# Products with stationary activations: down and output projections of a fused spiking-attention, FFN and attention block

## The chip, the cores and the metric

One core of one Trainium2 chip runs the kernel. The metric is the device time of the whole program in microseconds (us), the median of several runs; lower is better.

## The reference

The input x has 8 batches of 256 tokens of 128 features. Four blocks follow each other, each with a residual:

```
x = x + attn_a(layernorm(x))   # sigmoid projections, a matrix A from mean spike times, A @ V @ Wo + bo
x = x + ffn(layernorm(x))      # (silu(x wg) * (x wu)) wd, integer weights / 127
x = x + attn_b(layernorm(x))   # 16 heads of 64, causal softmax
x = x + ffn(layernorm(x))      # the same weights again
```

The two products that the change touches:

```
return jnp.einsum('bsh,dh->bsd', h, wd)            # ffn, h has 384 features: the down projection
out = jnp.einsum('bsha,had->bsd', z, Wo) + bo      # attn_b: the output projection
```

## The kernel before

All work is cut by batch b (0 to 7). Each batch goes through lnt and qkv, mean, vwo, aout (attn_a, letter A), lntF, gF0 to gF2, dnF, dbF (the first FFN, letter F), lntB, qk, v, scores, exp, transposes, sum, otA, otB, otr (attn_b, letter B; m = 8b + u counts the head pairs of all batches), and lntP, gP, dnP, dbP (the second FFN, letter P). Jobs of several batches are in flight together. Nothing schedules them at run time: `ORDER` is a table that lists, for each of TensorE, ScalarE, VectorE and GpSimd, every job in the order in which that engine runs it, and `BANKS` gives each job's PSUM bank. `full` waits until a job has filled its bank, `freed` until its reader has emptied it, `take` on TensorE until the bank's turn before is over. An engine that waits holds up everything behind it in its list. The SP queue loads x and stores each batch after dbP has been added (L392).

Much of the work on TensorE is done on values that are split in two fp32r parts, hi (rounded by ScalarE) and lo (the rest, by VectorE or GpSimd), for which a matmul is issued each time. `hot` jobs are four transposes of the identity with no result that is used.

Down projection (dnF, dnP; L463 to L471): the weight tile wd is stationary and 256 tokens of the hidden values stream past, hi and lo for each of the 3 chunks of features, six matmuls. Out come features on partitions and tokens on columns. ScalarE copies them to `dnt` (L690), and dbF or dbP (L486) turns them back by two transposes; VectorE then adds the result to x (L842). Two of the sixteen, F of batch 0 and P of batch 7 (`DIRECT`), take the hidden values as the stationary operand in plain fp32 (L480).

Output projection of batches 0 to 6: otA takes head pairs 0 to 3 and otB the pairs 4 to 7, three matmuls of 256 tokens for each pair:

```
nc.tensor.matmul(out[:, 0:N], wo_hi[:, u, :], z_hi, start=(u == 0), stop=False)
nc.tensor.matmul(out[:, 0:N], wo_lo[:, u, :], z_hi, start=False, stop=False)
last = nc.tensor.matmul(out[:, 0:N], wo_hi[:, u, :], z_lo, start=False, stop=(u == U - 1))
```

ScalarE copies the bank to `ot` (L700), otr transposes it twice (L534), VectorE adds it to x (L854). The last batch has its own product in plain fp32, tokens on partitions (pre0, pre1, out0, out1).

In the trace a plain fp32 product leaves two matmul records and two load records for each instruction, an fp32r product or a transpose one. Loads of the stationary operand are told as PEld.

## Time and profile before

| | |
|---|---|
| time, median of 3 runs | 320.98 us (320.28 to 321.02) |
| span of the profiled execution | 318.3 us |
| busy: TensorE, its loads | 307.6 us (97%), 268.4 us (84%) |
| busy: VectorE, ScalarE, GpSimd | 278.0 us (87%), 248.9 us (78%), 227.9 us (72%) |
| chain that ended last: TensorE, GpSimd, issue | 72%, 13%, 7% |

The profile shows one execution. Its own time is told as its span alone, from the first instruction to the last; the runs' median lies 2.7 us above it. A matmul's duration reaches from its start to the end of its last column, and the next one starts before that, so durations of TensorE don't add up; the distance from one start to the next does.

### The profile page before, as it was taken

To read this page: it belongs to the slowest core of one execution; us is meant where nothing else is said; L and a number is where in the kernel's file an instruction comes from. 1 tells how busy PE (TensorE), PEld (TensorE's weight loads), DVE (VectorE), ACT (ScalarE), POOL (GpSimd) and SP (SyncE) were. 2 spreads that over 40 slices of the span, in tenths; PEclk is the share of its full clock that TensorE was granted. 3 is DMA by queue.
4 is the path that set the end of the run, shared out by engine and by line. 5 is a ranking of instruction groups with operands and counts; after the bars stand their busy time and mean duration, and the time that the engine had idled before them with its cause. 6 is when DMAs were issued, how large, how long until landed. Compare 5 with 4: busy or idle time off the path is not lost.

```text
span 318.3 us, 10097 instructions
## 1 busy us (share of the span) xinstructions
PE 307.6 (97%) x3186; PEld 268.4 (84%) x3186; DVE 278.0 (87%) x1117; ACT 248.9 (78%) x848; POOL 227.9 (72%) x305
## 2 busy tenths in 40 slices
PE   6898999999999999999999999999999999999995
PEld 5687987988888898898888897888978998888884
DVE  4698999999899989997999989989998898998564
ACT  2665599899779798869889886998779788779832
POOL 4465786949978976977995489863977497646740
PEclk9999999999999999999999999999999999999999
DMA  7900000000000000000000000000000000000001
GB/s 201 316 7 0 3 0 4 2 3 1 2 2 2 2 2 4 0 3 3 18 2 3 3 16 3 2 18 3 2 1 4 19 0 21 2 2 4 2 0 49
DMA packets 6419, 5.83 MB, mean 18 GB/s; under 512 B 864, under 2 KB 5856, under 8 KB 6368
## 3 DMA queue, kind: packets, MB, share of 16 engines
q1 hardware_dynamic: 6080, 4.99, 5.2%
q8 instruction: 26, 0.43, 0.6%
q14 instruction: 25, 0.20, 0.2%
q10 hardware_dynamic: 288, 0.20, 0.2%
HBM read 4.15 MB, written 1.05 MB: 16 GB/s over the span
## 4 chain that ended last, share of the span: by engine, by line
PE 72%; POOL 13%; issue 7%; DVE 5%; DMA 1%; ACT 1%; POOLq 0%; DVEq 0%; ACTq 0%
PE bank L606 10%; PE bank L399 8%; PE bank L400 7%; PE bank L583 7%; PE bank L401 7%; PE bank L571 7%; POOL prob L1019 6%; PE bank L568 4%; PE bank L469 3%; PE bank L459 3%; PE bank L460 2%; PE bank L417 2%; PE bank L448 2%; PE bank L526 2%; PE bank L527 2%
## 5 line engine op out<-in xcount | busy, mean ns | idle before, releaser
L1019 POOL TENSOR_TENSOR prob<-prob,row_inv 128x256 f32<-128x256 f32 (+1 forms) x128 | 103.5, 838 | 33.9 <-DVE row_inv L921 33.8
L719 ACT ACTIVATE prob<-neg_s,neg_max 128x256 f32<-128x256 f32 x128 | 64.1, 501 | 0.0
L717 ACT ACTIVATE prob<-neg_s,neg_max 128x128 f32<-128x128 f32 x128 | 50.8, 397 | 13.8 <-DVE neg_max L897 13.2
L897 DVE CUSTOM_DVE_ANT_0 neg_s<-bank,mask 128x256 f32<-128x256 f32 x128 | 53.7, 420 | 0.0
L606 PE MATMUL bank<-early,v 128*64 128x256 f32 (+1 forms) x512 | 46.0, 330 | 0.1
L606 PEld LDWEIGHTS bank<-early,v 128*64 128x64 f32 x512 | 32.2, 137 | 13.1 <-issue 3.4
L931 DVE TENSOR_TENSOR qk<-bank,bqk 128x512 f32<-128x512 f32 x64 | 42.0, 681 | 0.9 <-PE bank L401 0.8
L571 PE MATMUL bank<-qk 64*128 64x256 f32 x256 | 38.6, 377 | 0.0
L895 DVE CUSTOM_DVE_ANT_0 neg_s<-bank,mask 128x128 f32<-128x128 f32 x128 | 36.4, 284 | 1.8 <-PE bank L571 1.7
L399 PE MATMUL bank<-rt_hi,wqkv_hi 128*128 128x256 f32 x128 | 37.2, 290 | 0.1
L400 PE MATMUL bank<-rt_hi,wqkv_lo 128*128 128x256 f32 x128 | 36.1, 282 | 0.0
L401 PE MATMUL bank<-rt_lo,wqkv_hi 128*128 128x256 f32 x128 | 36.1, 282 | 0.0
L906 DVE COPY early<-bank 128x384 f32<-128x384 f32 x64 | 32.9, 549 | 2.9 <-PE bank L583 2.8
L728 ACT ACTIVATE early<-bank 128x384 f32<-128x384 f32 x64 | 28.5, 488 | 7.6 <-PE bank L583 7.0
L583 PEld LDWEIGHTS bank<-ident,prob 64*128 64x128 f32 x768 | 27.7, 139 | 5.5 <-issue 2.2
L583 PE MATMUL bank<-ident,prob 64*128 64x64 f32 x768 | 30.9, 225 | 0.2 <-POOL prob L1019 0.2
L568 PE MATMUL bank<-qk 64*128 64x128 f32 x256 | 27.5, 291 | 0.2 <-issue 0.2
L568 PEld LDWEIGHTS bank<-qk 64*128 64x128 f32 x256 | 22.3, 187 | 4.5 <-issue 1.9
L399 PEld LDWEIGHTS bank<-rt_hi,wqkv_hi 128*128 128x128 f32 x128 | 24.3, 190 | 1.4 <-issue 0.5
L717 ACT ACTIVATION_READ_ACCUMULATOR prob<-neg_s,neg_max 128x1 f32 x128 | 24.8, 194 | 0.0
L400 PEld LDWEIGHTS bank<-rt_hi,wqkv_lo 128*128 128x128 f32 x128 | 24.3, 190 | 0.5
L719 ACT ACTIVATION_READ_ACCUMULATOR prob<-neg_s,neg_max 128x1 f32 x128 | 24.6, 192 | 0.0
(178 smaller groups left out, 887.2 us busy)
## 6 DMA issues: line engine op xcount, KB each, us to landing
early<-wqkv_in SPq DMA_DIRECT2D x3, 512.0 KB, 6.9
x<-x_in SPq DMA_DIRECT2D x8, 128.0 KB, 5.7
out<-x SPq DMA_DIRECT2D x8, 128.0 KB, 1.8
wo<-wo_in SPq DMA_DIRECT2D x1, 512.0 KB, 7.0
wa<-wa_in ACTq DMA_DIRECT2D x1, 192.0 KB, 3.1
first<-wg_in SPq DMA_DIRECT2D x1, 192.0 KB, 3.1
first<-wu_in SPq DMA_DIRECT2D x1, 192.0 KB, 3.1
first<-wd_in SPq DMA_DIRECT2D x1, 192.0 KB, 4.8
```

The costliest lines, as they stand in the source:

```text
L399: nc.tensor.matmul(out, w_hi_ap, r_hi_ap, start=True, stop=False)
L400: nc.tensor.matmul(out, w_lo_ap, r_hi_ap, start=False, stop=False)
L401: return nc.tensor.matmul(out, w_hi_ap, r_lo_ap, start=False, stop=True)
L568: nc.tensor.matmul(home(f"s{e}", m)[0][:, 0:P], qk[half, r, 0, 0:P], qk[half, r, 1, 0:P], start=True, stop=True)
L571: nc.tensor.matmul(S[:, P:SC], qk[half, r, 0, P:N], qk[half, r, 1, :], start=True, stop=True).then_inc(done, 1)
L583: last = nc.tensor.transpose(out[:, at:at + A], prob[half, m % PROB_BUFS, e, j * P:(j + 1) * P], ident[half, half])
L606: last = nc.tensor.matmul(out[half, t + k * P:t + N], v[:, b % 2, k, h * A:(h + 1) * A], transposed(i)[:, e, cols], start=(k == 0), stop=( ...
L717: nc.scalar.activation(prob[:, r, e, 0:P], neg_s[:, m % SCORE_BUFS, e, 0:P], ACT.Exp, bias=neg_max[:, q, 2 * e:2 * e + 1], scale=-1.0, acc ...
L719: nc.scalar.activation(prob[:, r, e, P:SC], neg_s[:, m % SCORE_BUFS, e, P:SC], ACT.Exp, bias=neg_max[:, q, 2 * e + 1:2 * e + 2], scale=-1. ...
L897: nc.vector.tensor_tensor_reduce(out=neg_s[:, m % SCORE_BUFS, e, P:SC], in0=S[:, P:SC], in1=mask[:], scale=-SCORE_SCALE, scalar=3e38, op0= ...
L931: nc.vector.tensor_tensor(qk[:, m % QK_BUFS, :, :], W[:].rearrange("p (w s) -> p w s", s=N), bqk[:, u, :].unsqueeze(2).to_broadcast([P, 2, ...
L1019: nc.gpsimd.tensor_tensor(pr, pr, inv, ALU.mult).then_inc(p_norm, 1)
```

## The change

The jobs dnF, dnP and otr are gone, with the copies of ScalarE and the tiles `dnt` and `ot`. dbF and dbP now wait for the split hidden values and compute the down projection themselves: for each half of the tokens and each chunk, the hi and the lo hidden tile is stationary (128 x 128) and wd streams with its 128 columns. otA and otB do the same with z_hi, z_lo as stationary tiles and wo_hi, wo_lo streaming. The results stand with tokens on partitions, and VectorE adds them to x from the bank. The hidden buffers are free for the next batch once db is done. All of ORDER and BANKS is new.

The end of TensorE's list, before, from the down projection of batch 6 of P (hid_hi_P) on:

```order
L469 MATMUL bank<-hid_hi_P,wd 128x256 x3
L469 MATMUL bank<-hid_lo_P,wd 128x256 x3
L486 MATMUL bank<-ident,dnt_P 128x128 x2
L499 MATMUL bank<-ident 128x128 x2
L500 MATMUL bank<-ident 128x128
L501 MATMUL bank<-ident 128x128
L486 MATMUL bank<-ident,dnt_P 128x128 x2
L480 MATMUL bank<-wd,hid_F 128x128 x6
```

The same place now:

```order
L487 MATMUL bank<-ident 128x128 x2
L488 MATMUL bank<-ident 128x128
L489 MATMUL bank<-ident 128x128
L473 MATMUL bank<-wd,hid_hi_P 128x128
L473 MATMUL bank<-wd,hid_lo_P 128x128
...
L464 MATMUL bank<-wd,hid_F 128x128 x6
```

The six wide matmuls and the transposes became twelve matmuls of 128 columns (the pair of L473 rows comes six times), and the projection of batch 5 left this place: it now stands between lntP.7 and gP0.7:

```order
L411 MATMUL bank<-ident,xn_F 128x128 x2
L473 MATMUL bank<-wd,hid_hi_P 128x128
L473 MATMUL bank<-wd,hid_lo_P 128x128
...
L453 MATMUL bank<-xt_hi_F,wg 128x256
```

GpSimd's list, before, around the split of the output weights (wo_lo), just ahead of the first output projection:

```order
L1003 TENSOR_TENSOR hid_lo_F<-hid_F,hid_hi_F 128x256
L1007 TENSOR_TENSOR wo_lo<-wo,wo_hi 128x1024
L991 TENSOR_SCALAR sv<-t_qkv 128x256
L986 TENSOR_TENSOR x<-x,bo_all 128x256
L1003 TENSOR_TENSOR hid_lo_F<-hid_F,hid_hi_F 128x256 x2
```

Now the split stands near the start of the kernel:

```order
L941 TENSOR_SCALAR xn_A<-x,mv_eps,rstd_A 128x128 x2
L978 TENSOR_TENSOR wo_lo<-wo,wo_hi 128x1024
L962 TENSOR_SCALAR sv<-t_qkv 128x256
L983 TENSOR_SCALAR stdp<-less 128x512
L967 TENSOR_TENSOR wqkv_lo<-early,wqkv_hi 128x512
L962 TENSOR_SCALAR sv<-t_qkv 128x256
```

It moved from after ten normalisations to before the first, and the splits of the query, key and value weights (wqkv_lo) now queue behind it.

```diff
@@ -49,148 +49,143 @@
 ORDER = {
     "PE": """
...
-        v3.0 scores.3 scores.4 scores.5 mean.2 v2.0 qk.6 dnF.1 qk.7 v0.0 dbF.1 transposes.0 transposes.1 transposes.2
...
 BANKS = {
-    "lntA": "43744110",
...
+    "lntA": "32277257",
...
-    "dnF": "06070106",
...
-    "ot": "5264737",
-    "otr": "3116311",
...
-    "dnP": "4514010",
...
+    "ot": "3362374",
...
@@ -281,7 +276,7 @@
         sv, tq, tk, vwo = sb("sv", [P, 2, N]), sb("tq", [P, 2, N]), sb("tk", [P, 2, T]), sb("vwo", [P, 2, T, D])
         dist, less = (sb(n, [P, T, N]) for n in ("dist", "less"))
         stdp, xb = sb("stdp", [P, 2, T, N]), sb("xb", [P, 2, T, D])
-        gate_t, hid, dnt = ({k: sb(f"{n}_{k}", [P, w, N]) for k in "FP"} for n, w in (("gate_t", FC), ("hid", FC), ("dnt", 1)))
+        gate_t, hid = ({k: sb(f"{n}_{k}", [P, FC, N]) for k in "FP"} for n in ("gate_t", "hid"))
         hid_hi, hid_lo = ({k: sb(f"{n}_{k}", [P, FC, N], F32R) for k in "FP"} for n in ("hid_hi", "hid_lo"))
         qk = sb("qk", [P, QK_BUFS, 2, N])
         v = sb("v", [P, 2, T, H * A])
@@ -291,7 +286,6 @@
         prob_t = early[:].rearrange("p (m e s) -> p m e s", m=PT_BUFS, e=2)
         zt_hi, zt_lo = sb("zt_hi", [P, Z_SLOTS, N], F32R), sb("zt_lo", [P, Z_SLOTS, N], F32R)
         wo_hi, wo_lo = sb("wo_hi", [P, U, D], F32R), sb("wo_lo", [P, U, D], F32R)
-        ot = sb("ot", [P, N])
         zt_last = first[:, 0:U * N].rearrange("p (u s) -> p u s", s=N)
 
         bank = [ctx.enter_context(nc.psum_tensor(f"bank{i}", [P, 512], F32)) for i in range(8)]
@@ -459,16 +453,6 @@
                         nc.tensor.matmul(out[:, cols], w[:, cs], xt_hi[buffers(k, b)][:, 0, :], start=True, stop=False)
                         last = nc.tensor.matmul(out[:, cols], w[:, cs], xt_lo[buffers(k, b)][:, 0, :], start=False, stop=True)
                     last.then_inc(done, 1)
-                elif job in ("dnF", "dnP"):
-                    k = job[2]
-                    for c in range(FC):
-                        pe.wait_ge(hl_s[k][c], turn_of(k, b))
-                    take(job, b)
-                    for half in (hid_hi, hid_lo):
-                        for c in range(FC):
-                            last = nc.tensor.matmul(out[:, 0:N], wd[:, c, :], half[k][:, c, :], start=(half is hid_hi and c == 0),
-                                                    stop=(half is hid_lo and c == FC - 1))
-                    last.then_inc(done, 1)
                 elif job in ("dbF", "dbP"):
                     k = job[2]
                     if (k, b) in DIRECT:
@@ -480,10 +464,14 @@
                                 last = nc.tensor.matmul(out[:, j * D:(j + 1) * D], hid[buffers(k, b)][:, c, j * P:(j + 1) * P], wd[:, c, :].bitcast(F32),
                                                         start=(c == 0), stop=(c == FC - 1))
                     else:
-                        freed(pe, f"dn{k}", b)
+                        for c in range(FC):
+                            pe.wait_ge(hl_s[k][c], turn_of(k, b))
                         take(job, b)
                         for j in range(T):
-                            last = nc.tensor.transpose(out[:, j * D:(j + 1) * D], dnt[k][:, 0, j * P:(j + 1) * P], ident[:])
+                            for c in range(FC):
+                                for half in (hid_hi, hid_lo):
+                                    last = nc.tensor.matmul(out[:, j * D:(j + 1) * D], half[k][:, c, j * P:(j + 1) * P], wd[:, c, :],
+                                                            start=(c == 0 and half is hid_hi), stop=(c == FC - 1 and half is hid_lo))
                     last.then_inc(done, 1)
                 elif job == "bo":
                     pe.wait_ge(bv_s, 1)
@@ -522,17 +510,13 @@
                     else:
                         freed(pe, "sum", U * b + U - 1)
                     for u in range(0 if first else U // 2, U // 2 if first else U):
-                        z_hi, z_lo = zt_hi[:, slot(b, u), :], zt_lo[:, slot(b, u), :]
-                        nc.tensor.matmul(out[:, 0:N], wo_hi[:, u, :], z_hi, start=(u == 0), stop=False)
-                        nc.tensor.matmul(out[:, 0:N], wo_lo[:, u, :], z_hi, start=False, stop=False)
-                        last = nc.tensor.matmul(out[:, 0:N], wo_hi[:, u, :], z_lo, start=False, stop=(u == U - 1))
+                        for j in range(T):
+                            z_hi, z_lo = (z[:, slot(b, u), j * P:(j + 1) * P] for z in (zt_hi, zt_lo))
+                            o = out[:, j * D:(j + 1) * D]
+                            nc.tensor.matmul(o, z_hi, wo_hi[:, u, :], start=(u == 0 and j == 0), stop=False, skip_group_check=True)
+                            nc.tensor.matmul(o, z_hi, wo_lo[:, u, :], start=False, stop=False, skip_group_check=True)
+                            last = nc.tensor.matmul(o, z_lo, wo_hi[:, u, :], start=False, stop=(u == U - 1), skip_group_check=True)
                     last.then_inc(ota_s if first else done, 1)
-                elif job == "otr":
-                    freed(pe, "ot", b)
-                    take(job, b)
-                    for j in range(T):
-                        last = nc.tensor.transpose(out[:, j * D:(j + 1) * D], ot[:, j * P:(j + 1) * P], ident[:])
-                    last.then_inc(done, 1)
                 elif job[0] == "v":
                     g, j = divmod(int(job[1]), T)
                     freed(pe, "lntB", b)
@@ -679,25 +663,12 @@
                     k, c = job[2], int(job[3])
                     freed(act, f"g{k}{c}", b)
                     if turn_of(k, b) > 1:
-                        full(act, f"dn{k}", b - 1)
+                        full(act, f"db{k}", b - 1)
                     nc.scalar.activation(hid_hi[k][:, c, :], hid[k][:, c, :], ACT.Copy).then_inc(hh_s[k][c], 1)
-                elif job in ("dnF", "dnP"):
-                    k = job[2]
-                    src, _, free = home(job, b)
-                    full(act, job, b)
-                    if turn_of(k, b) > 1:
-                        full(act, f"db{k}", b - 1)
-                    nc.scalar.activation(dnt[k][:, 0, :], src[:, 0:N], ACT.Copy).then_inc(free, 1)
 
                 elif job == "oh":
                     act.wait_ge(ld_b, 64)
                     nc.scalar.activation(wo_hi[:], wo[:], ACT.Copy).then_inc(woh_s, 1)
-                elif job == "ot":
-                    src, _, free = home(job, b)
-                    full(act, job, b)
-                    if b:
-                        full(act, "otr", b - 1)
-                    nc.scalar.activation(ot[:], src[:, 0:N], ACT.Copy).then_inc(free, 1)
                 elif job == "dist":
                     act.wait_ge(mean_s, b + 1)
                     if b:
@@ -772,7 +743,7 @@
                     if k == "A":
                         dve.wait_ge(ld_x[b], 16)
                     elif k == "P" and b < B - 1:
-                        freed(dve, "otr", b)
+                        freed(dve, "ot", b)
                     elif k == "P":
                         freed(dve, "out0", b)
                         freed(dve, "out1", b)
@@ -847,7 +818,7 @@
                     full(dve, job, b)
                     dve.wait_ge(xbo_s, b + 1)
                     nc.vector.tensor_tensor(x[:, j, :], src[:, 0:D], x[:, j, :], ALU.add).then_inc(free, 1)
-                elif job == "otr":
+                elif job == "ot":
                     src, _, free = home(job, b)
                     full(dve, job, b)
                     dve.wait_ge(xbo_s, b + 1)
@@ -999,7 +970,7 @@
                     k, c = job[2], int(job[3])
                     pool.wait_ge(hh_s[k][c], turn_of(k, b))
                     if turn_of(k, b) > 1:
-                        full(pool, f"dn{k}", b - 1)
+                        full(pool, f"db{k}", b - 1)
                     nc.gpsimd.tensor_tensor(hid_lo[k][:, c, :], hid[k][:, c, :], hid_hi[k][:, c, :].bitcast(F32), ALU.subtract).then_inc(hl_s[k][c], 1)
 
                 elif job == "ol":
```

## Rows read from the trace of the kernel before

**Rows 1.** the page of the profile: span, busy time of each engine, clock, the chain by engine

```profile
span 318.3 us, 10097 instructions
...
PE 307.6 (97%) x3186; PEld 268.4 (84%) x3186; DVE 278.0 (87%) x1117; ACT 248.9 (78%) x848; POOL 227.9 (72%) x305
...
PEclk9999999999999999999999999999999999999999
...
PE 72%; POOL 13%; issue 7%; DVE 5%; DMA 1%; ACT 1%; POOLq 0%; DVEq 0%; ACTq 0%
```

**Rows 2.** groups of instructions by form, TensorE: line, operation, tiles, count, busy us, mean ns

```profile
L526 PE MATMUL bank<-zt_hi,wo_hi 128*128 128x256 f32 x56 | 16.1, 288 | 0.3 <-POOL wo_lo L1007 0.3
...
L469 PE MATMUL bank<-hid_hi_F,wd 128*128 128x256 f32 x21 | 3.9, 296 | 0.0
...
L534 PE MATMUL bank<-ident,ot 128*128 128x128 f32 x14 | 2.8, 284 | 0.0
```

**Rows 3.** timeline of TensorE, sixth output projection: start us, us, engine, line, form

```profile
252.13 0.28 PE L526 MATMUL bank<-zt_hi,wo_hi 128*128 128x256 f32 x1
...
254.88 0.28 PE L528 MATMUL bank<-zt_lo,wo_hi 128*128 128x256 f32 x1
```

**Rows 4.** timeline of TensorE, a down projection of the second FFN near the end

```profile
306.25 0.52 PE L469 MATMUL bank<-hid_hi_P,wd 128*128 128x256 f32 x3
...
306.60 0.52 PE L469 MATMUL bank<-hid_lo_P,wd 128*128 128x256 f32 x3
...
306.96 0.28 PE L459 MATMUL bank<-xt_hi_P,wg 128*128 128x256 f32 x1
```

**Rows 5.** timeline of TensorE, transposes of the identity near the end

```profile
308.63 0.38 PE L499 MATMUL bank<-ident 128*128 128x128 f32 x2
...
308.85 0.27 PE L500 MATMUL bank<-ident 128*128 128x128 f32 x1
```

**Rows 6.** timeline around a mean's product: TensorE's matmuls, then its weight loads

```profile
44.15 0.50 PE L432 MATMUL bank<-mean_w,t_qkv 128*128 128x1 f32 x4
...
44.51 0.49 PE L399 MATMUL bank<-wqkv_hi,rt_hi 128*128 128x512 f32 x1
...
44.84 0.40 PE L400 MATMUL bank<-wqkv_hi,rt_lo 128*128 128x512 f32 x1
...
45.07 0.40 PE L401 MATMUL bank<-wqkv_lo,rt_hi 128*128 128x512 f32 x1
...
44.48 0.19 PEld L399 LDWEIGHTS bank<-wqkv_hi,rt_hi 128*128 128x128 f32 x1
...
44.60 0.19 PEld L400 LDWEIGHTS bank<-wqkv_hi,rt_lo 128*128 128x128 f32 x1
```

**Rows 7.** timeline, the direct down projection at the end, weight loads

```profile
313.95 1.41 PEld L480 LDWEIGHTS bank<-wd,hid_F 128*128 128x128 f32 x12
```

**Rows 8.** groups of instructions by form, ScalarE: count, busy us, mean ns

```profile
L690 ACT ACTIVATE dnt_F<-bank 128x256 f32<-128x256 f32 x7 | 2.7, 382 | 1.4 <-PE bank L469 1.4
...
L700 ACT ACTIVATE ot<-bank 128x256 f32<-128x256 f32 x7 | 2.7, 382 | 1.5 <-PE bank L528 1.5
```

**Rows 9.** the chain that ended last: start us, us, what

```profile
74.47 2.38 POOL wo_lo L1007
...
311.96 0.94 PE bank L469 x6
...
313.75 0.41 PE bank L486 x2
...
314.16 1.41 PE bank L480 x12
```

**Rows 10.** timeline of the probabilities' loads, a weight split of GpSimd, TensorE's fifth query/key product

```profile
296.65 1.81 PEld L583 LDWEIGHTS bank<-ident,prob 64*128 64x128 f32 x48 [0.17 <-issue]
...
21.68 1.29 POOL L996 TENSOR_TENSOR wqkv_lo<-early,wqkv_hi 128x512 fp32r<-128x512 f32 x1
...
37.69 0.28 PE L399 MATMUL bank<-rt_hi,wqkv_hi 128*128 128x256 f32 x1
```

More of the change, by code:

```diff
@@ L81 @@
[L81 to L82 removed]
+        hot.0 hot.1 hot.2 hot.3 hot.4 hot.5 hot.6 hot.7 hot.8 lntA.0 qkv1.0 qkv0.0 qkv2.0 mean.0 hot.9 hot.10 hot.11 hot.12
+        lntA.1 vwo.0 aout.0 hot.13 hot.14 qkv1.1 qkv0.1 qkv2.1 lntF.0 mean.1 gF0.0 gF2.0 gF1.0 bo.0 lntA.2 dbF.0 qkv2.2 qkv1.2
+        vwo.1 vwo.2 aout.1 lntB.0 qkv0.2 qk.0 qk.1 qk.2 scores.0 scores.1 scores.2 lntF.1 qk.3 qk.4 gF0.1 gF1.1 gF2.1 v1.0 qk.5
@@ new lines @@
+        v0.0 scores.3 scores.4 scores.5 transposes.0 mean.2 qk.6 qk.7 dbF.1 v3.0 transposes.1 lntA.3 transposes.2 sum.1
+        transposes.3 scores.6 scores.7 v2.0 aout.2 lntB.1 sum.3 qkv1.3 qk.8 qk.9 qk.10 v3.1 qk.11 v0.1 transposes.4 transposes.5
+        transposes.6 transposes.7 scores.8 scores.9 scores.10 qkv0.3 qk.12 qkv2.3 qk.13 lntF.2 sum.5 scores.11 gF2.2 v1.1 gF1.2
+        sum.7 scores.12 scores.13 qk.14 mean.3 gF0.2 otA.0 otB.0 qk.15 vwo.3 transposes.8 transposes.9 dbF.2 v2.1 transposes.10
@@ new lines @@
+        scores.14 scores.15 transposes.11 sum.9 sum.11 lntA.4 lntB.2 aout.3 transposes.12 v2.2 qk.16 qk.17 qk.18 v0.2
+        transposes.13 scores.16 scores.17 sum.13 lntP.0 lntF.3 qk.19 v1.2 gP2.0 v3.2 gF1.3 transposes.14 transposes.15 scores.18
+        scores.19 qkv2.4 gF2.3 gF0.3 qkv1.4 sum.15 qk.20 qk.21 qkv0.4 qk.22 transposes.16 transposes.17 scores.20 scores.21
+        scores.22 dbF.3 gP1.0 gP0.0 otA.1 lntA.5 transposes.18 transposes.19 mean.4 otB.1 qk.23 lntB.3 sum.17 qk.24 vwo.4 qk.25
@@ new lines @@
+        transposes.20 transposes.21 scores.23 scores.24 scores.25 sum.19 sum.21 lntP.1 qk.26 qk.27 aout.4 v0.3 gP2.1 v1.3 dbP.0
+        qkv2.5 gP1.1 transposes.22 transposes.23 scores.26 transposes.24 scores.27 qk.28 qk.29 lntF.4 v2.3 qkv0.5 qk.30 qk.31
+        gF1.4 qkv1.5 gP0.1 scores.28 transposes.25 mean.5 gF2.4 gF0.4 otA.2 vwo.5 scores.29 sum.23 sum.25 scores.30 lntA.6 dbF.4
+        otB.2 qkv2.6 aout.5 transposes.26 transposes.27 scores.31 dbP.1 v3.3 lntB.4 sum.27 v2.4 qk.32 qk.33 transposes.28
@@ new lines @@
+        v1.5 gF2.6 qk.43 gF0.6 gP0.3 transposes.38 transposes.39 dbP.2 gF1.6 sum.37 sum.39 transposes.40 transposes.41 scores.42
+        scores.43 gP1.3 qkv1.7 qk.44 qk.45 dbF.6 qk.46 mean.7 scores.44 scores.45 gP2.3 qk.47 otA.4 otB.4 v3.5 vwo.7 lntB.6
+        scores.46 transposes.42 transposes.43 sum.41 transposes.44 scores.47 transposes.45 sum.43 aout.7 qk.48 qk.49 v1.6 lntP.4
+        scores.48 scores.49 qk.50 gP2.4 v2.6 qk.51 gP0.4 lntF.7 dbP.3 sum.45 transposes.46 transposes.47 scores.50 scores.51
```

232 lines of the change are left out of this document (106 added, 126 removed).

## The prediction

> **What bounds the kernel now.** I read the page's busy shares and chain first [rows 1]. TensorE is busy 97% of a span of 318.3 us, at the full granted clock all the way; VectorE follows at 87%, ScalarE at 78%, GpSimd at 72%. The busy share of TensorE overstates it, since the matmuls' durations overlap, but the chain that ended last says the same: 72% of it is TensorE's work, 13% GpSimd's, 7% "issue", and ScalarE's share is 1%. So a change is priced first by what it does to TensorE's stream.
>
> A duration in the groups [rows 2] is no price: a matmul of 256 columns is listed at 288 ns, but starts follow each other much more closely. The price is the distance from one start to the next (pitch). In one output projection 24 matmuls run unbroken, the first at 252.13, the last at 254.88: 2.75 us over 23 steps, **0.120 us** each [rows 3]. In one down projection six of them take from 306.25 to the next job's start at 306.96: **0.118 us** each [rows 4]. Transposes of 128 columns (here of the identity, the same form) come every **0.110 us**: two from 308.63 to 308.85 [rows 5].
>
> **The change, part by part.** Both products are turned round: the activations are the stationary operand, so the tokens come out on partitions and nothing is transposed back. The activation tile that is loaded has 128 tokens where 256 streamed, so each matmul of 256 columns becomes two of 128: 24 become 48 in each of seven output projections, 6 become 12 in each of fourteen down projections (batches 1 to 7 of F, 0 to 6 of P; the two direct ones stay). Two transposes for each of the 21 go. In all 504 matmuls of 128 columns stand where there were 168 + 84 of 256 columns and 42 transposes [rows 2].
>
> What one of the new ones costs is the question of this case, because no reduced-precision (fp32r) matmul here streams fewer than 256 columns. Nearest rows, from both sides:
> - Streaming alone. The 512-column matmuls of the value projection have a pitch of 0.23 us (44.84 to 45.07) [rows 6], against 0.120 at 256 columns. The straight line through both gives 0.120 - 0.5 x 0.11 = 0.063 us at 128 columns. That is the lower end.
> - Loading alone. Four matmuls of the mean stream **one** column each and still need 0.36 us from 44.15 to 44.51, 0.09 us each, where streaming would need next to nothing; and the two fp32r loads behind them start at 44.48 and 44.60, 0.12 apart [rows 6]. The direct down projection, 128 columns in full fp32, runs its twelve loads in 1.41 us, of which the last one's own duration is 0.19: (1.41 - 0.19)/11 = 0.111 us [rows 7].
> - The upper end of the same mechanism is today's 0.120 us: a narrower stream can't be slower than a wider one of its kind.
>
> So a new 128x128 load every matmul sets the pitch, and halving the columns buys nothing. I take **0.112 us** (that of the direct projection, the nearest in shape, rounded up) and keep 0.120 as the high end.
>
> Output projection: 48 x 0.112 = 5.38 us; before 24 x 0.120 + 2 x 0.110 = 3.10. Plus 2.28, seven times: **+15.9 us**. Down projection: 12 x 0.112 = 1.34; before 6 x 0.118 + 2 x 0.110 = 0.93. Plus 0.41, fourteen times: **+5.8 us**. Together +21.7. At 0.120 it is 2.66 x 7 + 0.51 x 14 = +25.8.
>
> The Trainium skill, "TensorE: Matmul & The Clock Gate", section "Back-to-back issue gap", gives a sustained spacing of about 81 ns for pairs of load and matmul at 128 columns. By it the 504 would take 40.8 us, and TensorE's work would grow by 6.1 us instead of 21.7. The loads here come no closer than 0.11 us [rows 6, 7], so the trace speaks for the dearer figure.
>
> ScalarE loses 21 evacuations of 382 ns [rows 8], 8.0 us of its 248.9. It holds 1% of the chain, so this is worth nothing by itself. The cover is TensorE's queue, and TensorE gets longer. VectorE still adds each result to x from a bank (the same 21 instructions), now released by the projection itself. The chain of a projection gets shorter by an evacuation and two transposes; in the middle of the kernel the engine runs another job meanwhile, so this hop was hidden. 21 turns of banks fewer are needed, which can only ease the waits for a bank. The SP queue's stores wait on the same job as before.
>
> At the end it isn't hidden. From 311.96 the chain holds six matmuls (0.94), two transposes, and an evacuation with its hops up to 313.75, two more transposes (0.41), then the direct projection at 314.16: 2.20 us [rows 9]. Now twelve matmuls stand there: 1.34 + about 0.2 of start, 1.6 us; the twelve of the batch before moved ahead of the last gate products, where TensorE turned idle matmuls over while it waited for a split. **-0.5 us**.
>
> The orders: GpSimd's split of the output weights (wo_lo) was on the chain at 74.47 for 2.38 us just ahead of the first projection [rows 9]; it moves into the first 25 us. There a copy of sv, a step of stdp and two weight splits queue behind it; the first of these splits ran at 21.68, and TensorE first reads it at 37.69 [rows 10], so 2.4 us more are covered (without that cover they would be paid in full). That is worth 0 to 2.4; I take **-1.0**, because other work of GpSimd takes its place on the chain. All other moves are small and of both signs, I give them 0 with 2 us on either side.
>
> **How much of +21.7 reaches the end.** If TensorE were the whole chain, all of it. It is 72% [rows 1]; the other 28% are waits on normalisation, splits and issue, and part of them is covered once TensorE runs later than the others. With the chain's share as the lower rate, 15.6; with all of it, 21.7. The inserted blocks themselves are unbroken TensorE work on the chain [rows 3, 9], so I take it nearer to the full rate, 20.3. Sum: 20.3 - 0.5 - 1.0 = **+18.8 us**. On the profiled span that is 318.3 + 18.8 = 337.1; the runs' median of 320.98 lies 2.7 above the span, and the difference carries over: **339.8 us**.
>
> **Rivals.**
> 1. *Half-width reduced matmuls run as plain fp32.* Every 128-column product in this trace is plain fp32 and leaves two matmul records for each instruction (12 in the chain's last row for the direct projection's six [rows 9]), 0.224 us for the pair. Should the single pass hold only for wide tiles, 504 x 0.224 = 112.9 us against 34.7 before: +78.2, with the credits of 1.5 some 398 us. For it: no narrow fp32r matmul exists here to say otherwise. Against it: records are split by type, and both widths that are shown take one. Chance 0.10.
> 2. *The loads hide, and streaming decides* (the other side). Place: every load of the 504. Price: at the 0.063 us of the straight line 31.8 us against 34.7, -2.9; with -0.5 and -1.0 it comes to 316.6 us. It decides from a pitch of 34.7/504 = 0.069 us down. For it: the 48 loads of the probabilities' transposes, on half the rows each, come every 0.04 us [rows 10], and two matmuls in each three of the output projection hold the same stationary tile. Against it: the one-column rows, and the tail's identity transposes, which repeat the same tile and still come at 0.110 [rows 5]. Chance 0.07. The skill's formula in that same section, columns over 2.4 GHz plus 2.5 ns, would make it 56 ns and 28.2 us, so faster still by 3.6 us; the one-column rows, at a multiple of it, do not agree.
> 3. *Only the repeated tile is kept.* A third of the 336 output matmuls (112) would skip the load: 112 x (0.112 - 0.063) = -5.5 us, 334.3 us. Inside the range, by part of the main case.
> 4. *The waits swallow it.* TensorE grows but VectorE and GpSimd were due anyway: two thirds of 21.7 vanish in today's waits, 7.2 - 1.5 = +5.7, 326.7 us. For it: VectorE's 87%. Against it: the chain is at VectorE in only 5% [rows 1]. Chance 0.07.
>
> **Numbers.** Load-bound, as worked out (rival 3 within it): 0.76, between 329 (pitch 0.112, chain's rate 15.6, the moves at their best, the repeated tile kept: 15.6 - 5.5 x 0.72 - 0.5 - 2.4 - about 1 = +8) and 347 (25.8 in full, no credit). To hold 8 in 10 the range reaches down to rival 4's 326. About 0.3% is what a measurement of this kernel can tell from no change, that is 320.0 to 321.9. Faster: rival 2, 0.07. Within: edges of rivals 2 and 4, 0.03. Slower: the rest, 0.90.
>
> **What the profile after would show.** 504 matmuls of 128x128 at the two projections, each with its own load; a pitch of 0.11 to 0.12 in an unbroken block (5.4 us for 48, where 2.9 stood); no matmul or activation on the lines that are gone; TensorE's share of the chain up by some points; ScalarE's busy time near 241 us; wo_lo off the chain. A pitch at or under 0.07, or two records for each instruction, proves the step wrong, and then rival 2 or 1 holds. A pitch of 0.112 with a span under 327 would leave the step of the rate at fault.

## The result, and the profile after

The changed kernel takes **343.65 us** (median of 4 runs, 343.19 to 344.35) beside 321.0 for the kernel before on the same chip: a ratio of 1.0714, 95% interval 1.0702 to 1.0727. It is slower by 22.7 us; 339.8 was forecast, with a range of 326 to 347.

The page of the changed kernel, where [rows 1] stood before:

```profile
span 341.4 us, 10455 instructions
...
PE 328.3 (96%) x3396; PEld 288.6 (85%) x3396; DVE 278.4 (82%) x1117; ACT 245.8 (72%) x827; POOL 227.7 (67%) x305
...
PE 89%; POOL 5%; issue 2%; DVE 2%; ACT 1%; POOLq 0%; DVEq 0%; ACTq 0%
```

TensorE was 72% of the chain that ended last and is 89% now. The span grew by 23.1 us, TensorE's busy time by 20.7; the other engines do what they did (ScalarE 3.1 us less) and are idle for longer. TensorE's clock is granted in full all the way (1.00).

The groups by form, matmuls and then weight loads (these answer to [rows 2]):

```profile
L517 PE MATMUL bank<-wo_lo,zt_hi 128*128 128x128 f32 x112 | 30.8, 275 | 0.0
...
L473 PE MATMUL bank<-wd,hid_hi_P 128*128 128x128 f32 x42 | 9.8, 276 | 0.5 <-POOL hid_lo_P L974 0.5
```

```profile
L517 PEld LDWEIGHTS bank<-wo_lo,zt_hi 128*128 128x128 f32 x112 | 21.5, 192 | 0.0
```

Three such groups of 112 and four of 42 make the 504. One record stands for each instruction, so these products run as a single pass and not as plain fp32. L517 follows L516 with the same stationary tile z_hi and still has its own 112 loads.

The timeline of TensorE through the first output projection gives the price (before: [rows 3]); 48 matmuls, the last one followed by a query/key product:

```profile
78.92 0.22 PE L516 MATMUL bank<-wo_hi,zt_hi 128*128 128x128 f32 x1
78.98 0.28 PE L517 MATMUL bank<-wo_lo,zt_hi 128*128 128x128 f32 x1
79.09 0.27 PE L518 MATMUL bank<-wo_hi,zt_lo 128*128 128x128 f32 x1
79.20 0.28 PE L516 MATMUL bank<-wo_hi,zt_hi 128*128 128x128 f32 x1
...
84.12 0.28 PE L518 MATMUL bank<-wo_hi,zt_lo 128*128 128x128 f32 x1
84.23 0.33 PE L393 MATMUL bank<-rt_hi,wqkv_hi 128*128 128x256 f32 x1
```

From 78.92 to 84.23 are 5.31 us for 48: a pitch (the distance from one start to the next) of **0.111 us**, though each duration is listed as 275 ns. A down projection near the end runs from 330.92 to 332.29, 1.37 us for twelve. Per projection that is 5.31 - 3.10 = 2.21 us more, seven times 15.5; and 1.37 - 0.93 = 0.44 us more, fourteen times 6.2. Together 21.7, the sum that the prediction had for TensorE. It is scaled up from one block of each kind; a count of all blocks, further down, comes to 20.6.

The waits of the other engines, by what they wait for:

```profile
POOL prob L990 <- DVE row_inv L892: 48.3, 29, 5.6
ACT early L699 <- PE bank L567: 18.9, 20, 2.7
...
DVE x L825 <- PE bank L518: 11.6, 7, 3.3
```

GpSimd's first wait was 33.8 us before and ScalarE's wait for the transposes 7.0; VectorE now waits up to 3.3 us for an output projection. These three engines stand idle for longer in all, and 89% of the chain is TensorE's.

Where the time is added shows in four marks, read off the timelines in us: the start of TensorE's first scores, of its first output projection, of its last sum product, and from that to the end.

| kernel | first scores | first output projection | last sum | tail |
|---|---|---|---|---|
| before | 33.84 | 76.89 | 301.21 | 17.06 |
| changed | 34.76 | 78.92 | 323.61 | 17.78 |

The tail is what is left behind the start of the last sum product. Up to the first scores 0.9 us are added, from there to the first output projection 1.1, from there to the last sum product 20.4, in the tail 0.7.

### The profile page after: what moved, and what is told of

Read it like the earlier page. It is cut to its first block, busy times and chain, and to the rows that moved or that the text cites. A ratio compares the mean times of both kernels' runs of the same rounds, so it can differ in the third digit from the quotient of the medians.

```text
span 341.4 us, 10455 instructions
## 1 busy us (share of the span) xinstructions
PE 328.3 (96%) x3396; PEld 288.6 (85%) x3396; DVE 278.4 (82%) x1117; ACT 245.8 (72%) x827; POOL 227.7 (67%) x305
## 4 chain that ended last, share of the span: by engine, by line
PE 89%; POOL 5%; issue 2%; DVE 2%; ACT 1%; POOLq 0%; DVEq 0%; ACTq 0%
PE bank L590 13%; PE bank L393 8%; PE bank L567 8%; PE bank L555 8%; PE bank L394 7%; PE bank L395 7%; PE bank L473 6%; PE bank L552 5%; PE bank L518 4%; PE bank L517 4%; PE bank L516 4%; PE bank L453 3%; PE bank L454 3%; PE bank L411 2%; PE bank L442 2%
## 5 line engine op out<-in xcount | busy, mean ns | idle before, releaser
L590 PE MATMUL bank<-early,v 128*64 128x256 f32 (+1 forms) x512 | 46.7, 330 | 0.1
L902 DVE TENSOR_TENSOR qk<-bank,bqk 128x512 f32<-128x512 f32 x64 | 42.8, 685 | 4.3 <-PE bank L395 3.7
L699 ACT ACTIVATE early<-bank 128x384 f32<-128x384 f32 x64 | 29.2, 488 | 19.4 <-PE bank L567 18.9
L393 PE MATMUL bank<-rt_hi,wqkv_hi 128*128 128x256 f32 x128 | 37.9, 296 | 0.6 <-DVE rt_lo L839 0.6
L877 DVE COPY early<-bank 128x384 f32<-128x384 f32 x64 | 33.6, 551 | 5.2 <-PE bank L567 4.6
L567 PE MATMUL bank<-ident,prob 64*128 64x64 f32 x768 | 32.1, 226 | 0.0
L518 PE MATMUL bank<-wo_hi,zt_lo 128*128 128x128 f32 x112 | 30.8, 275 | 0.0
L517 PE MATMUL bank<-wo_lo,zt_hi 128*128 128x128 f32 x112 | 30.8, 275 | 0.0
L516 PE MATMUL bank<-wo_hi,zt_hi 128*128 128x128 f32 x112 | 30.5, 272 | 0.0
L552 PEld LDWEIGHTS bank<-qk 64*128 64x128 f32 x256 | 21.7, 187 | 4.8 <-issue 3.1
```

What stands on the lines that cost most here:

```text
L393: nc.tensor.matmul(out, w_hi_ap, r_hi_ap, start=True, stop=False)
L517: nc.tensor.matmul(o, z_hi, wo_lo[:, u, :], start=False, stop=False, skip_group_check=True)
L552: nc.tensor.matmul(home(f"s{e}", m)[0][:, 0:P], qk[half, r, 0, 0:P], qk[half, r, 1, 0:P], start=True, stop=True)
L567: last = nc.tensor.transpose(out[:, at:at + A], prob[half, m % PROB_BUFS, e, j * P:(j + 1) * P], ident[half, half])
L590: last = nc.tensor.matmul(out[half, t + k * P:t + N], v[:, b % 2, k, h * A:(h + 1) * A], transposed(i)[:, e, cols], start=(k == 0), stop=( ...
```

## The experiments

Each is given as its edit, what was expected, what was measured, and what follows. Times are medians; ratios are to the kernel before on the same chip, with their 95% interval.

### Is it the load? Smaller loads against narrower streams

Two edits of the changed kernel leave its 504 matmuls and all orders alone. One halves what is loaded (64 tokens, A = 64), the other halves what streams.

```diff
-   matmul(out[:, j * D:(j + 1) * D], half[k][:, c, j * P:(j + 1) * P], wd[:, c, :], ...)
+   matmul(out[0:A, j * D:(j + 1) * D], half[k][:, c, j * P:j * P + A], wd[:, c, :], ...)   # e4, z_hi and z_lo alike
+   matmul(out[:, j * D:j * D + D // 2], half[k][:, c, j * P:(j + 1) * P], wd[:, c, 0:D // 2], ...)   # e5, wo_hi and wo_lo alike
```

**Half the load (e4).**

> The changed kernel with 64 instead of 128 tokens in each stationary tile of the 504, streaming 128 columns as changed; it leaves out the other 64 tokens of each tile. Load theory: the load halves, the pitch falls from 0.112 to the streaming value of about 0.063 us: -24.7 us on TensorE, 319 to 325 us, and the pitch in a block is 0.06 to 0.07. Rival, a fixed cost for each matmul (issue) of 0.112 whatever it loads: 343 to 344 us and an unchanged pitch.

Measured 319.06 us (318.88 to 319.17), ratio 0.9958 [0.9943, 0.9972]: 24.6 us less than the changed kernel. The timeline of the same place:

```profile
79.20 0.22 PE L516 MATMUL bank<-wo_hi,zt_hi 128*64 128x128 f32 x1
79.26 0.23 PE L517 MATMUL bank<-wo_lo,zt_hi 128*64 128x128 f32 x1
79.32 0.22 PE L518 MATMUL bank<-wo_hi,zt_lo 128*64 128x128 f32 x1
```

With the same count and the same 128 columns the pitch fell from 0.111 to 0.06 us, and the time stands at the low edge of what was expected if the load decides. 504 x 0.051 = 25.7 us of TensorE, and 24.6 of it came off the time. Whether the smaller load or the 128 columns set the 0.06 can't be told: the straight line for the stream alone lies at nearly the same place.

**Half the stream (e5).**

> The changed kernel streaming only 64 of the 128 weight columns in each of the 504 matmuls, with the full 128x128 tile loaded each time; it leaves out half of the features of both products. Load theory: nothing changes, 343.0 to 344.3 us, pitch 0.11. Rival, the stream still decides some of the pitch (half of 504 x 0.056): 14 us less, 329 us; it decides at once between load and stream, as e4 did between load and issue.

Measured 362.92 us, and from 355.67 to 367.35 over the runs at a mean granted clock of 0.93 to 0.96; the ratio for the two runs at 0.95 and 0.96 is 1.1153 [1.1113, 1.1193]. The expectation was missed by far, but not by its mechanism. The timeline of the first block, and three stretches around it (length, each engine's busy time, then the granted clock before the DMA share):

```profile
79.40 0.28 PE L517 MATMUL bank<-wo_lo,zt_hi 128*128 128x64 f32 x1
79.51 0.28 PE L518 MATMUL bank<-wo_hi,zt_lo 128*128 128x64 f32 x1
...
81.52 0.28 PE L518 MATMUL bank<-wo_hi,zt_lo 128*128 128x64 f32 x1
...
81.97 0.40 PE L518 MATMUL bank<-wo_hi,zt_lo 128*128 128x64 f32 x1
82.19 0.40 PE L516 MATMUL bank<-wo_hi,zt_hi 128*128 128x64 f32 x1
```

```profile
79.30:81.70 2.40, 2.40 (x25) 2.40 (x23) 2.33 (x9) 2.21 (x7) 2.31 (x4) 1.00 0.00 0
81.70:98.80 17.10, 17.10 (x109) 15.54 (x108) 6.62 (x24) 6.12 (x22) 7.87 (x12) 0.50 0.00 1
98.80:110.00 11.20, 11.20 (x126) 9.20 (x124) 9.83 (x44) 7.98 (x26) 7.84 (x11) 1.00 0.01 1
```

Up to 81.5 us, at the full 2.4 GHz, the pitch is 0.11 us (79.40 to 81.52 in 19 steps, 0.112): half the columns bought nothing. Then, inside the block, the clock is granted at its half level (1.2 GHz), the pitch doubles to 0.21, and it stays so for 17.1 us. This happens seven times in the run. An estimate of what the clock took: time at half rate is half lost, so a run loses (1 - mean granted clock) x span, and without it the four spans come to 339.7 to 340.1 us, close to the changed kernel's 341.4. So the pair of runs says: **the load of a 128x128 stationary tile sets the pitch; neither the stream nor the issuing of an instruction does.** The clock is taken up again below.

### Is it the count, or the new orders?

**Cut in two (e2).** The kernel before with its own orders, banks and orientation; only each matmul of 256 columns at the two products is cut into two of 128.

```diff
-   matmul(out[:, 0:N], wo_hi[:, u, :], z_hi, ...)
+   for j in range(T):
+       matmul(out[:, j * P:(j + 1) * P], wo_hi[:, u, :], z_hi[:, j * P:(j + 1) * P], ...)   # and so the others
```

> The kernel before, orders, banks, copies and transposes untouched; each wide matmul of both products is cut in two of 128 streamed columns (weights stationary as before, loaded twice). Pitch theory: 504 x 0.112 = 56.4 us for 168 x 0.120 + 84 x 0.118 = 30.1 us, +26.3 us on TensorE, at nine tenths to the full rate: 345 to 347 us. Rival, that the orders carry the loss: well under 335 us. Streaming as the limit: 504 x 0.063 = 31.8, so 323 us.

Measured 345.26 us (345.12 to 345.36), ratio 1.0775 [1.0757, 1.0793]: +24.9. As expected: with nothing moved and nothing turned round, cutting alone costs more than the whole change does. The new orders are not the main cause.

**Half of the new matmuls (e3), and half of those of the down projections (e6).** The changed kernel with `for j in range(1)` in place of `range(T)`: in both products, and in the down projections alone.

> The changed kernel with the second half of the tokens left out of both products (252 of the 504 new matmuls), all other jobs, orders and banks as changed. It leaves out half of the down and output projections' results. Pitch theory: -28.2 us on TensorE, so 343.7 falls by 20 to 28, to 316 to 324 us (TensorE then has 6.5 us less to do than before, and other engines can bind). Rival, that orders or banks carry the loss: above 332 us.

> The changed kernel with the second half of the tokens left out of the fourteen down projections alone (84 of 168 matmuls). Pitch theory, at the rate of 0.96 that e3 showed for all 252: 84 x 0.112 x 0.96 = -9.0 us, 334.6 us (+-1). Rival: down projections stand where TensorE waits anyway, so much of it vanishes: above 338 us.

Measured 316.62 us (315.98 to 317.12), ratio 0.9881 [0.9863, 0.9899], and 334.1 us (333.88 to 334.5), ratio 1.0433 [1.042, 1.0447]. The first takes away 27.0 us for 252 x 0.112 = 28.2 of TensorE's work, 0.96 of it; the second 9.5 for 84 x 0.112 = 9.4, all of it. Both are inside what was expected. In e3's profiled run the clock stood at half from 306.3 to 309.7 us, and its tail is 17.78 us where e6's is 16.64, so 0.96 is rather too low. So nearly every microsecond that these blocks take arrives at the end.

**The output projection alone (e1).** The kernel before, with only otA and otB turned round as in the change (its bank row for ot new, ot's places on VectorE and the halves' places on TensorE moved by a few jobs); the down projections stay wide.

```diff
-    "ot": "5264737",
+    "ot": "1124337",
```

> The kernel before with the output projection alone turned round (48 matmuls of 128 columns for 24 of 256, otr and its copy gone); the down projections as before; before's orders with only the ot jobs' banks and places shifted so that the banks come free. Theory of TensorE's pitch: +2.28 us seven times, +15.9 us, nearly all of it at the end: 335 to 338 us. Rival, that the new orders and banks carry the loss: these are nearly the old ones here, so under 330 us.

Measured 340.26 us (339.89 to 340.46), ratio 1.0618 [1.0603, 1.0634]: +19.9, where its term is 15.5 to 15.9: above the range that was expected, by some 2 us, and 4 above the term. Its marks up to the first output projection (33.80, 76.86) and its tail (17.05) are those of the kernel before, so all of it arises in the middle. There TensorE's listed idle time rises from 0.5 to 2.1 us; where the rest of the 4 us arises was not located.

**The same, with half its matmuls (e11).**

```diff
-                        for j in range(T):
+                        for j in range(1):
```

> The kernel e1_out_only (output projection alone turned round, the orders of before with its new places and banks) with the second half of the tokens left out of the seven output projections, so half of their matmuls (168) are gone; rows 128 to 255 of each batch get wrong sums. TensorE then does 24 x 0.112 = 2.69 us per projection where before did 3.10, 2.9 us less in seven. Theory A, the 4 us that e1_out_only cost beyond its term are a fixed price of the places and banks that were patched for it: 340.3 less 0.95 to 1.0 of 18.8, so 321.4 to 322.5 us. Theory B, they arise only with the long blocks themselves (each holds up work on other engines that comes back late): with short blocks they vanish, 317.9 to 319.0 us, below before.

Measured 326.26 us (324.75 to 329.28), ratio 1.0176 [1.014, 1.0212]; the runs at full clock took 324.75 and 324.88. Theory B is refuted: with blocks shorter than those of the kernel before, this version is still slower than it. That speaks for the places and banks patched for e1. But A's fixed price of 4 us isn't shown either: its range was missed upward by more than 2 us, since taking matmuls away gave back 15.5 of 18.8 at full clock and no more, so that the price here would be nearer 7. What e1 costs beyond its term stays open in part. The down projections alone, on the orders of before, were not tried.

### The tail

The forecast had -0.5 us for the end on top of what the two down projections there add (0.8), so +0.3; it is +0.7. The changed kernel's timeline there, TensorE, ScalarE and GpSimd, with the idle time ahead in brackets:

```profile
330.71 0.44 PE L411 MATMUL bank<-ident,xn_F 128*128 128x128 f32 x2 [1.01 <-DVE xn_F L767]
...
332.55 0.73 ACT L667 ACTIVATE hid_hi_P<-hid_P 128x256 fp32r<-128x256 f32 x2 [0.98 <-PE bank L473]
...
333.40 2.11 POOL L974 TENSOR_TENSOR hid_lo_P<-hid_P,hid_hi_P 128x256 fp32r<-128x256 f32 x3 [3.39 <-ACT hid_hi_P L667]
...
335.77 0.30 PE L473 MATMUL bank<-wd,hid_hi_P 128*128 128x128 f32 x1 [0.52 <-POOL hid_lo_P L974]
```

There is one set of hidden tiles for P. Before, they were free once dnP of batch 5 had run, ahead of batch 6's gates. Now dbP of batch 5 reads them itself, at 330.92 to 332.29, and ScalarE's rounding for batch 6 waits for it (0.98 us), GpSimd's split waits for the rounding (3.39), and TensorE, which turns idle transposes over meanwhile, still waits 0.52.

**Batch 5's projection earlier (e7).**

```diff
-  gP1.6 hot.15 gP0.6 gP2.6 lntP.7 dbP.5 gP0.7
+  gP1.6 dbP.5 hot.15 gP0.6 gP2.6 lntP.7 gP0.7
```

> The changed kernel with the down projection of P batch 5 moved on TensorE from behind lntP.7 to behind gP1.6. Theory: batch 6's rounding (hid_hi_P) now waits until that projection has read the buffers, and through GpSimd's splits the last two projections start late; moved, dbP.6 starts about 1.2 us and dbP.7 about 1.0 us earlier: 342.4 to 342.9 us. Rival, the tail is bound by the last batch's own chain (xn, gates): 343.5 or above.

Measured 345.04 us (343.93 to 345.8), ratio 1.0771 [1.0752, 1.0789]; tail 18.10 against 17.78. The theory is a miss: the edit made it worse, and the time lies in the rival's range. Of the 0.7 us that the profiled span grew, 0.4 were there at the first output projection (79.34 against 78.92), far ahead of the edit: the clock stood at half for 3.4 us near the start (see the last section). The tail's share is 0.3, and TensorE's timeline shows why it got no shorter.

```profile
333.51 0.39 PE L453 MATMUL bank<-xt_hi_F,wg 128*128 128x256 f32 x1 [1.86 <-DVE xt_lo_F L839]
...
336.51 0.30 PE L473 MATMUL bank<-wd,hid_hi_P 128*128 128x128 f32 x1
```

Dropped ahead of the gates of batch 6, dbP of batch 5 pushes them back, and with them the work of ScalarE and VectorE that stands ahead of batch 7's normalised input (xt_lo). TensorE now waits 1.86 us for it at 333.51; in the changed kernel it was ready at 332.02, and its gates started at 332.29, right behind dbP of batch 5. The wait on the split is gone, but dbP of batch 6 starts 0.7 us later than it did. So most of that block of 1.3 us had filled a wait in its old place, and the edit took it out of there.

**The other way out (e9): batch 6 direct in the kernel before.** Down projection of P batch 6 in plain fp32 from the unsplit hidden values, as batch 7's; its rounding, split, copy and transposes back go, and it moves ahead of dbP of batch 5.

```diff
-DIRECT = {("F", 0), ("P", B - 1)}
+DIRECT = {("F", 0), ("P", B - 2), ("P", B - 1)}
-  gP0.7 gP1.7 gP2.7 dnP.6 dbP.5 hot.18 dbP.6 dbP.7
+  gP0.7 gP1.7 gP2.7 dbP.6 dbP.5 hot.18 dbP.7
```

> The kernel before with the down projection of P batch 6 made direct (plain fp32, hidden values stationary, no rounding, split, copy or transposes; six matmuls between the last gate products and the end). Theory: near the end the chain goes through GpSimd's splits of batch 6 (308.45 to 311.96) and a copy and two transposes; without them the last projection starts 0.5 to 0.9 us earlier: ratio 0.997 to 0.9985. Rival: the last batch's gates set the end, ratio 1.000.

Measured 320.09 us (319.75 to 320.51, 11 runs) beside 320.61 (21 runs), ratio 0.999 [0.9981, 0.9999]: hardly to be told from no change, and a little less than expected. Its chain ends so:

```profile
311.62 1.34 PE bank L480 x12
312.96 0.22 PE bank L486 x2
...
313.84 1.59 PE bank L480 x12
```

The chain no longer passes through a split or an evacuation behind the last gates. What lies between the two direct projections is TensorE's own queue: the two transposes back of batch 5 (L486) and the idle ones. Note the 1.34 us: six plain fp32 instructions, with twelve loads, take TensorE as long as the changed kernel's twelve matmuls on split values, without the split.

### The split of the output weights

The prediction moved wo_lo off the chain and credited 1.0 us. The chain of the changed kernel, in the head:

```profile
22.10 1.58 POOL xn_A L941 x2
23.69 2.34 POOL wo_lo L978
...
26.93 0.62 POOL stdp L983
27.55 1.24 POOL wqkv_lo L967
```

It is on the chain still. Behind it wait sv, stdp and the weight splits on GpSimd, and from there the chain goes on through the normalisations to TensorE at 37.06. Two runs put it elsewhere.

**Back to its old place (e8).**

```diff
-  lnsF.0 lnsA.2 ol.0 sv.1 ... norm.9 hlF2.2 xb.4
+  lnsF.0 lnsA.2 sv.1 ... norm.9 hlF2.2 ol.0 xb.4
```

> The changed kernel with GpSimd's split of the output weights moved back to where the kernel before has it (behind norm.9). Theory A: in the changed kernel it lies on the chain at 23.7 us for 2.3 us and delays the first heads by some 0.9 us; back in its place it costs the middle instead, where TensorE has more to do than before and hides it: 342.5 to 343.2 us. Theory B, that the move was worth the 1.0 us that the prediction gave it: 344.2 to 345 us.

Measured 351.79 us (350.68 to 355.15), ratio 1.1012 [1.0971, 1.1053]. Both theories missed, by some 7 us or more. TensorE's timeline, then stretches as above:

```profile
81.59 0.33 PE L506 MATMUL bank<-wo_hi,zt_hi 128*128 128x128 f32 x1 [2.12 <-POOL wo_lo L968]
...
83.43 0.28 PE L507 MATMUL bank<-wo_lo,zt_hi 128*128 128x128 f32 x1
...
83.66 0.41 PE L506 MATMUL bank<-wo_hi,zt_hi 128*128 128x128 f32 x1
83.88 0.41 PE L507 MATMUL bank<-wo_lo,zt_hi 128*128 128x128 f32 x1
```

```profile
80.00:83.60 3.60, 2.01 (x18) 2.01 (x19) 2.23 (x6) 3.45 (x11) 3.51 (x5) 1.00 0.00 0
83.60:93.90 10.30, 10.30 (x66) 9.96 (x65) 2.21 (x4) 0.70 (x3) 3.38 (x5) 0.50 0.01 2
93.90:110.00 16.10, 16.10 (x179) 13.31 (x179) 14.27 (x67) 12.16 (x41) 13.43 (x18) 1.00 0.01 2
```

TensorE stands still for 2.12 us, then runs a block of 128x128 loads with 128 columns each; after 2.0 us of it the clock is granted at half, and 10.3 us pass at half rate, the block's pairs at a pitch of 0.21. The same block without the wait ahead of it kept the full clock in the changed kernel. The wait costs 2 us, and half of the 10.3 us, 5, is the clock's. The marks agree: of the 7.5 us that the profiled span grew, 0.3 lie ahead of the first scores (35.10), 2.3 between them and the first output projection (81.59), and 4.8 between that and the last sum (331.12).

**Into an idle stretch (e12).**

```diff
-  lnsF.0 lnsA.2 ol.0 sv.1 ... norm.7 lnsF.2 norm.8
+  lnsF.0 lnsA.2 sv.1 ... norm.7 lnsF.2 ol.0 norm.8
```

> The changed kernel with GpSimd's split of the output weights moved out of the head into the stretch from 66.4 to 72.0 us in which GpSimd waits 5.60 us for a reciprocal (behind lnsF.2). Theory A, the split delays the head by 0.9 us and nothing waits for it here: 342.5 to 343.2 us, the milestone of the first scores back at 33.9 and no wait on wo_lo at the first output projection, so no fall of the clock there, other than in e8_wo_lo_back. Theory B, without the split in the head TensorE's clock falls to half near 22 us as in e8_wo_lo_back, which eats the gain: 343.3 to 344.5 us.

Measured 343.38 us (342.69 to 343.45), ratio 1.071 [1.0695, 1.0724], which can't be told from the changed kernel's 1.0714. The first scores start at 34.20, 0.56 earlier, and the first output projection at 78.43, 0.49 earlier, with no wait; GpSimd's timeline shows the split inside the old idle stretch, which was 5.60 us long:

```profile
65.85 2.39 POOL L978 TENSOR_TENSOR wo_lo<-wo,wo_hi 128x1024 fp32r<-128x1024 f32 x1
71.49 1.61 POOL L990 TENSOR_TENSOR prob<-prob,row_inv 128x256 f32<-128x256 f32 x2 [3.25 <-DVE row_inv L892]
```

Of the 0.9 us of the head a little more than half comes back. The median lies where B put it and not where A did, but B's mechanism is not there: the clock is 0.999 in the profiled run and 1.000 in the four others. A was right in kind and too large: the span is 0.5 us shorter than the changed kernel's, and the medians, 0.3 apart, can't tell it. Beside e8 the run shows that taking the split out of the head was not what cost 8 us there: the loss came with the wait for it and the fall of the clock behind that wait.

### A version that beats both (e10)

e9, and the same move of wo_lo into the kernel before, where GpSimd waits 4.07 us behind lnsF of batch 2:

```diff
-  norm.7 lnsF.2 norm.8 lnsA.4 norm.9
+  norm.7 lnsF.2 ol.0 norm.8 lnsA.4 norm.9
```

> As e9, and GpSimd's split of the output weights moved from behind norm.9 to behind lnsF.2, into 4.07 us in which GpSimd sat idle. Theory: the 2.38 us that it held on the chain at 74.47 go, and other work takes part of it: 0.5 to 2.4 us less than e9, ratio 0.990 to 0.997. Rival: the work behind it takes its place on the chain, no difference from e9.

Measured **319.72 us** (319.31 to 319.83, 11 runs) beside 320.61, ratio 0.9972 [0.9963, 0.9981]: faster than both kernels, by 0.9 us than the one before. It is 0.37 us below e9, where 0.5 to 2.4 was expected, so a little short of the range. The first output projection starts at 76.44, before it was 76.89; but from there to the last sum product it takes 224.7 us where the kernel before took 224.3, and what is left of the profiled gain is e9's shorter tail (16.71 against 17.06). The page's chain:

```profile
PE 91%; DVE 4%; issue 1%; DMA 1%; POOL 1%; ACT 1%; POOLq 0%; DVEq 0%
```

GpSimd's 13% of the chain [rows 1] are down to 1%, and the time fell by 0.3%: nearly all of GpSimd's share had lain beside TensorE's own work, which now stands on the chain instead.

## Why the prediction was right, point by point

**What bounds the kernel.** Right: TensorE's stream. e3 and e6 took away matmuls and got 0.96 to 1.0 of them back.

**The price of a new matmul, 0.112 us.** Right: 0.111 in the block, and e4 against e5 shows the reason given to be the true one. The nearest row had been the direct projection, 0.111 [rows 7]. All 21 projections of the changed kernel, each counted from its first matmul to the next job's, take 56.3 us, where 504 x 0.112 are 56.4.

**Output and down projections, +15.9 and +5.8.** From one block of each kind the measured growth is 15.5 and 6.2, and that sum agrees with the 21.7. Counted in the same way over all blocks of both traces, the output projections go from 20.7 to 37.4 us and the down projections from 10.6 to 18.9, and 4.4 us of transposes are gone: **+20.6**, and TensorE's busy time says +20.7. What was there before had been priced at 34.7 and took 35.7, since many of its blocks run less tightly than the two that were read: the sum was 1.1 us too high.

**The Trainium skill**, "TensorE: Matmul & The Clock Gate", section "Back-to-back issue gap", would have had 81 ns for such a pair at 128 columns. At full clock 48 of them came at 0.111 each; the measurement decides. The same page's section "LDWEIGHTS (loading the stationary operand)" takes a load's columns divided by 1.2 as its nanoseconds, by which a load of 128 columns is an estimated 107 ns and one of 64 half of that. The pitches of 0.111 and, in e4, 0.06 lie a little above both.

**How much reaches the end.** Undersized. The prediction took 20.3 of 21.7 (0.935), between the chain's share of 72% and all of it. The chain's share was the wrong guide. In the long middle of the kernel before, TensorE is listed as idle for 0.5 us of 224.3, and in the changed kernel for none (each engine's busy time, TensorE's first):

```profile
76.89:301.21 224.32, 223.82 (x2429) 194.71 (x2429) 203.07 (x826) 188.11 (x658) 170.68 (x226) 1.00 0.02 5
```

```profile
78.92:323.61 244.69, 244.69 (x2653) 215.06 (x2651) 204.95 (x827) 187.18 (x645) 170.81 (x226) 1.00 0.02 5
```

The work that others did on the chain lay beside TensorE's, as e10 shows again, so what is added to TensorE there arrives in full. The blocks between these marks add 19.6 us, and their distance grew by 20.4; e3 and e6 gave back 0.96 to 1.0. That 20.3 was forecast for the products and 20.6 measured is luck in part: a sum 1.1 us too high met a rate too low.

**wo_lo, -1.0, and the other moves, 0.** Wrong, and the largest miss. The first output projection started 2.0 us later, of which the longer down projection of batch 1 of F ahead of it makes 0.2 (1.29 us where 1.04 stood); so the moves cost 1.8 us where 1.0 was credited, **2.8 us**. The split moved along the chain and not off it. Its first reader behind it, 16 us later [rows 10], had been taken for the only one that waits; the path that ends last ran on through GpSimd's own queue (sv, stdp, the weight splits). e12 brought 0.5 us of it back by moving the split alone; which of the other moves cost the rest was not taken apart. In the middle another **0.8 us** came that isn't the products' (20.4 less 19.6), where the moves had been given 0.

**The tail, -0.5.** The tail grew by 0.7 us, and its two longer projections make 0.8 of that, so about nothing was saved where 0.5 had been credited: **0.4 us**. The stretch that the step had priced did become shorter, from 2.20 us to 1.52, between the start of batch 6's projection (335.77) and the direct one on the chain; but these numbers already hold the longer projection, whose growth stands in the 21.7 as well. The sum charged those 0.4 us twice; without that the step would have missed by 0.8. What it missed lies ahead of that stretch: from the last sum product to the start of batch 6's projection are 12.2 us now and were 10.8, and the chain there now runs through the projection of batch 5 into the rounding. The step overlooked the new holder of the hidden tiles, though the diff shows it, in the waits for `db` where `dn` stood. e7 shows that the obvious cure costs more.

The terms with their misses give 18.8 + 0.3 (20.6 for 20.3) + 2.8 + 0.8 + 0.4 = 23.1, the growth of the span; the medians are 22.7 apart.

**The copies of ScalarE, 0.** Right: it is 1% of the chain as before. Its busy time fell by 3.1 us, not by 8.0 to near 241. The 21 copies are gone all the same: the durations of its instructions sum to 324.6 us before and 317.1 now, 7.5 less. They overlap one another, and busy time counts an overlapped stretch once.

**The rivals.** Plain fp32 (1): refuted by one record for each instruction and by the pitch. Streaming decides (2): refuted by e5's pitch at full clock. e4 came near its time with a smaller load, 319.06. Its straight line was misadded, too: 0.120 - 0.5 x 0.11 is 0.065 us and not 0.063, which would have made 317.5 of the rival's 316.6. The repeated tile kept (3): refuted, L517 has its own loads and the distance from L516 to L517 is the same 0.11. The waits swallow it (4): refuted by e2, e3 and e6.

## What to carry to other kernels

Price matmuls by the distance between starts, and ask at each whether the load of the stationary tile or the stream sets it: a 128x128 load costs 0.11 us whether 64, 128 or (0.120) 256 columns follow, so turning a product round so that a 256-wide side becomes the stationary one nearly doubles its cost (20.7 to 37.4 us for the seven output projections), and the saved transposes (0.22 us for each job) and copies don't pay for it. To tell how much of an added block will arrive, look how long TensorE is idle in that stretch, and not at its share of the chain. When an intermediate copy goes, look for who holds its source buffer now, and for whom that engine's next jobs wait. When a job is moved into an early place, follow what queues behind it on its own engine, not only its reader.

## What the runs showed of the hardware that was not expected

TensorE's granted clock fell from 2.4 to 1.2 GHz (1.00 to 0.50) several times inside a stretch in which the engine was listed as busy without a break. In e5 (64 columns for each 128x128 load) it fell at 81.7 us, in a block begun at 79.4 with no wait ahead; in e8 (128 columns) at 83.6, in a block begun at 81.6 behind a wait of 2.12 us; in the changed kernel and in e12, with the same block and no wait, it did not fall. In e11's profiled run it fell at 78.8 us, inside a wait of 1.01 us behind 12 such matmuls, and stayed down for about 10 us; in e3's it was down from 306.3 to 309.7. At half clock the pitch of these pairs is 0.213 us, so a product that is bound by loads is doubled too. The head of e7 and e8 shows a fall too, from 21.9 to 25.3 us in e7's profiled run, among matmuls of 256 columns, where the changed kernel ran the same jobs at full clock with nearly the same waits ahead; why one slipped and the other not stays open. e8 differs from the changed kernel and e12 in the place of the split alone, so the fall at 83.6 goes with the wait; but no run varied the length of the wait, or the columns behind one, so what brings a fall on is not shown.

```profile
21.90:25.30 3.40, 3.40 (x18) 3.40 (x18) 3.19 (x8) 1.96 (x6) 3.40 (x3) 0.50 0.02 7
```

```profile
21.90:25.30 3.40, 3.40 (x30) 3.28 (x30) 3.26 (x10) 2.85 (x8) 3.29 (x4) 1.00 0.03 7
```

The first is e7's stretch, the second the changed kernel's: 18 matmuls where there were 30, both listed as busy for all of it. A busy share of 100% says neither that the clock is full nor that the array is used.
